# Row moments and the convolution's product set between B products on VectorE, and seven tanh set ahead of two copies on ScalarE

## The reference, cut to what matters

```
xn   = x * rsqrt(mean(x*x) + 1e-6) * norm_w
proj = xn @ W_in.T                       # x_branch (512), gate (512)
xc   = conv(x_branch, 4 taps) + conv_b
xc   = xc * sigmoid(xc)
dt   = soft_clamp(softplus(xc @ W_dt.T + b_dt), 0.001, 0.1, 0.5)
Bp, Cp = xc @ W_B.T, xc @ W_C.T          # 16 states each
dA   = exp(soft_clamp(dt * A, -8, 8, 0.5))
# over time t, for every (channel, state):
h    = h * dA[t] + dt[t] * Bp[t] * xc[t]
h    = h * min(20 / (norm(h) + 1e-8), 1) if t % 10 == 0
y[t] = sum over states(h * Cp[t]) + D_param * xc[t]
x    = layernorm(x + x + scale * ((y * gate * sigmoid(gate)) @ W_out.T))
```

## Time and profile before

| | us |
|---|---|
| three timed runs, median (lowest to highest) | 2796.52 (2795.47 to 2802.35) |
| the profiled execution | 2795.66 |
| its span, first to last instruction | 2793.6 |
| TensorE busy | 2601.1 (93%) |
| VectorE busy | 2397.1 (86%) |
| ScalarE busy | 2245.1 (80%) |
| GpSimd busy | 2132.6 (76%) |

### The profile page before, as it was taken

How to read it: one execution, slowest core, us unless ns; L and a number is a source line. 1 busy time by engine, 2 the same in 40 slices (tenths; PEclk the granted TensorE clock), 3 DMA queues, 4 the chain that set the end, 5 groups by cost and what they waited for, 6 DMA issues and landing times. The chain is left out here.

```text
span 2793.6 us, 50775 instructions
## 1 busy us (share of the span) xinstructions
PE 2601.1 (93%) x16812; PEld 2390.9 (86%) x16812; DVE 2397.1 (86%) x3391; ACT 2245.1 (80%) x5074; POOL 2132.6 (76%) x2237
## 2 busy tenths in 40 slices
PE   5899999999999999999999999999999976899992
PEld 4799999999999999999999999999999975677762
DVE  2899999999999999999999999999999997221224
ACT  5899999999999999999999999999999971111113
POOL 0788888888888888888888888888888883434314
PEclk9899999999999999999999999999999987999996
DMA  1222222222222222222222222222222222134226
GB/s 61 69 73 80 83 70 80 78 75 82 70 84 80 75 81 73 78 83 72 79 78 76 82 70 84 78 76 82 72 78 79 72 79 96 42 98 102 61 49 252
DMA packets 145746, 225.65 MB, mean 81 GB/s; under 512 B 37836, under 2 KB 84684, under 8 KB 144332
## 3 DMA queue, kind: packets, MB, share of 16 engines
q1 hardware_dynamic: 123044, 188.95, 22.1%
q0 software_dynamic: 9216, 12.59, 2.6%
q10 hardware_dynamic: 13224, 20.86, 2.2%
HBM read 189.27 MB, written 33.05 MB: 80 GB/s over the span
## 5 line engine op out<-in xcount | busy, mean ns | idle before, releaser
L792 POOL TENSOR_TENSOR H<-H,CB 128x640 f32<-128x640 f32 (+1 forms) x832 | 1216.8, 1477 | 199.9 <-DVE H L610 199.8
L610 DVE TENSOR_TENSOR_SCAN H<-DA,PM 128x704 f32<-128x704 f32 (+1 forms) x832 | 1309.9, 1595 | 0.0
L514 ACT ACTIVATE DA<-DT,SM 128x160 f32<-128x160 f32 (+1 forms) x3328 | 1107.0, 422 | 1.6 <-POOL DT L754 0.3
L815 PE MATMUL YB<-H,ID 128*128 128x160 f32 (+1 forms) x6656 | 1043.9, 309 | 0.0
L815 PEld LDWEIGHTS YB<-H,ID 128*128 128x128 f32 x6656 | 982.4, 191 | 16.0 <-issue 11.2
L579 DVE TENSOR_TENSOR PM<-PM,BB 128x640 f32<-128x640 f32 (+1 forms) x832 | 674.0, 810 | 0.0
L377 ACT ACTIVATE DA<-DA 128x2560 f32<-128x2560 f32 (+1 forms) x206 | 477.8, 2320 | 1.7
L821 PE MATMUL PAZ<-XN,RB 128*128 128x160 f32 x1664 | 254.9, 307 | 0.9 <-DVE VV L684 0.9
L831 PEld LDWEIGHTS PAZ<-XB,CD 128*128 128x128 f32 x1664 | 237.5, 188 | 16.8
L765 POOL TENSOR_TENSOR FC<-SN,HALF 128x4 f32<-128x4 f32 x206 | 232.9, 1130 | 21.3 <-DVE SN L617 7.1
L840 PE MATMUL PAZ<-XC,RB 128*128 128x160 f32 x1664 | 243.0, 299 | 3.9 <-DVE XC L645 3.9
(11 more groups left out here) (157 smaller groups left out, 2816.3 us busy)
## 6 DMA issues: line engine op xcount, KB each, us to landing
BB<-Bd SPq DMA_DIRECT2D x208, 320.0 KB, 3.4
CB<-Cd SPq DMA_DIRECT2D x208, 320.0 KB, 3.2
W<-in_w ACTq DMA_DIRECT2D x16, 1024.0 KB, 7.8
XT<-in_xT SPq DMA_DIRECT2D x52, 160.0 KB, 2.2
XR<-in_xp SPq DMA_DIRECT2D x208, 40.0 KB
X2d<-VV SPq DMA_DIRECT2D x208, 40.0 KB
YA<-VV SPq DMA_DIRECT2D x208, 40.0 KB
HI<-YA SPq DMA_DIRECT2D x6, 1024.0 KB, 9.9
```

The lines of the kernel that those rows point to most:

```text
L514: eng.activation(DA[:, c0 + k0:c0 + k1, :, a, m, 1:11].rearrange("p c b t -> p b c t"), DT[:, j % 2, a].rearrange("p b (c t) -> p b c t", ...
L610: eng.tensor_tensor_scan(H[:, q % 3, u, 0:n], decays(c, g)[:, u], DBX(u)[:, 0:n], 0.0, ALU.mult, ALU.add).then_inc(s_scan, 1)
L792: eng.tensor_tensor(h, h, cb, ALU.mult).then_inc(s_hc, 1)
L815: mm = eng.matmul(yv, ID[:], hv[:, :, :, n, 0:w], start=False, stop=n == 15)
```

## The change

Three edits, all in `ssm_phase`. The first changes ScalarE's table: step 0 deals seven tanh instead of three, and step 2 three instead of seven, so four tanh move ahead of the two copies of step 1. The second puts the first B product of a step in front of XC in step 6, where XC stood ahead of both. The third moves the row moments out of step 13: `bn_stats` stands in step 14 behind the first B product, and `bn_aggr` behind the second. GpSimd's, TensorE's and SyncE's programs stay as they are.

```diff
-            DUE = [0, 3, 3, 10, 12, 18, 19, 27, 35, 41, 43, 50, 56, 56, 58, 64, 64]
+            DUE = [0, 7, 7, 10, 12, 18, 19, 27, 35, 41, 43, 50, 56, 56, 58, 64, 64]
...
                     q = 4 * i + r
+                    if live and u % 2 == 0:
+                        mult(q, u)
                     if s == 6 and ok(i + 2):
                         j = i + 2
                         eng.wait_ge(s_th, j + 1)
...
+                    if s == 14 and ok(i - 1):
+                        j = i - 1
+                        eng.wait_ge(s_v, j + 1)
+                        for g in range(2):
+                            eng.bn_stats(BN[:, g], VV[:, g]).then_inc(s_bn, 1)
                     if live and u % 2 == 0:
-                        mult(q, u)
                         carry(q, u)
                         mult(q, u + 1)
+                    if s == 14 and ok(i - 1):
+                        eng.wait_ge(s_bn, 2 * i)
+                        if i > 1:
+                            eng.wait_ge(s_sd, i - 1)
+                        for g in range(2):
+                            eng.bn_aggr(MVR[:, g], BN[:, g]).then_inc(s_mv, 1)
                     if u == 2 and 1 <= q <= NQ - 2:
                         norm_sum(q - 1)
...
-                        eng.wait_ge(s_v, j + 1)
-                        for g in range(2):
-                            eng.bn_stats(BN[:, g], VV[:, g]).then_inc(s_bn, 1)
-                        eng.wait_ge(s_bn, 2 * (j + 1))
-                        if j > 0:
-                            eng.wait_ge(s_sd, j)
-                        for g in range(2):
-                            eng.bn_aggr(MVR[:, g], BN[:, g]).then_inc(s_mv, 1)
```

## The result

The changed kernel takes 2855.29 us (median, 2853.9 to 2857.11), the kernel before 2796.37 us in the same comparison: a ratio of 1.0206, with a 95% interval of 1.0189 to 1.0224. That is slower, as forecast, but by 59 us and not by 36; 2832 was too low and the range ended at 2848. The profiled execution took 2857.11 us, its span is 2855.0.

What follows compares the result with a forecast made beforehand. VectorE was taken to bound the kernel, with GpSimd's path from bn_aggr to CAR setting the time after the change: 2795.66 + 51.0 - 11.7 - 3.8 + 0.5 = 2831.7, or 2832 us; range 2822 to 2848.

Steps and rivals of the forecast that it cites:

- The bound: State-space pass of 43.25 us: VectorE, busy 43.18, has no room; ScalarE is level with it within 0.08 us.
- The stall at the copy of CAR: Step 0 of the next pass: VectorE waits 1.04 us for GpSimd's CAR, 49 times, 51.0 us.
- The gaps: VectorE's waits at bn_stats, bn_aggr and XC go: 0.31 us a pass saved, 15.5 us together.
- The rule of the Trainium skill that the prediction weighed: Rival at bn_stats and bn_aggr: waits cost nothing extra, so 11.7 us are not saved; 2844 us, chance 0.06.
- XC and the seven tanh: Step 6: XC no longer waits for ScalarE's tanh, covered by ScalarE's idle time; 0.08 us a pass, 3.8 us saved.
- GpSimd makes its 1.4 us up by step 4: GpSimd, 1.4 us later after the move, recovers from its 5.25 us of idle time; nothing is charged.
- The 0.5 us added for the end of the stage: Pass 51: short products put bn_aggr and the last two products of H some 0.5 us later; bounds 0 and 0.6.
- The upper bound of 2836: Top of the main forecast, 2829 to 2836 us by the bounds of hand-over and end, given chance 0.70.
- GpSimd's path to CAR: Rival: FC at step 14 meets the larger price, 0.2 us more in 49 passes; 2842 us, chance 0.10.
- TensorE waits 0.68 us a pass for XN: Projection starts some 0.6 us later, covered by 1.66 us of room; rival without cover: 2881 us, chance 0.04.
- The 0.69 us by which CAR came early: Before the change, VectorE reached the copy of CAR 6.32 us after bn_aggr, GpSimd's path took 5.63: 0.69 us to spare.

## Why the prediction was right and wrong

- **The bound.** VectorE's order sets the pass, before and after. Right: in every run the pass is VectorE's own work and what holds VectorE.
- **The stall at the copy of CAR.** Right in place, cause, size and number: VectorE idles 49.2 us in 50 passes, one of which is the wait of pass 51 that was there before (1.17 us; 1.16 now). That leaves 48.1 us in 49 passes, 0.98 each. With the 0.08 us by which the copy would start before the end of the product in front of it, it comes 1.06 us later, against 1.04. Earlier `bn_aggr` shortens it one for one.
- **The gaps.** 0.31 us a pass were expected, 0.36 are gone from VectorE's row starts (VV to the next row 0.69 to 0.58, the second `bn_stats` to the next 0.44 to 0.33, XC 0.08, the rest in the rows behind the moments). The rule of the Trainium skill that the prediction weighed (VectorE: DVE Perf Modes, "The DRAIN you can't avoid"), by which the waits cost nothing extra, doesn't hold in this case: the instruction behind VV starts 0.11 us sooner when it doesn't need VV. The same section also says that a next instruction that is not held starts earlier, and that agrees with the rows that start 0.08 to 0.09 us before an end.
- **XC and the seven tanh.** Right that ScalarE's idle time covers the tanh and that XC's wait goes. But the 0.08 us of a pass came back as a port wait in step 6 (0.50 to 0.57 us), and the 4 us that the two edits give lie mostly in passes 0 and 1, which I hadn't priced. The sum of 3.8 us was about right for another reason.
- **The step that failed** is "GpSimd makes its 1.4 us up by step 4 [...] I charge nothing for these". GpSimd was followed for who *waits* for it by semaphore: TensorE, ScalarE, the next CAR. All that held. It wasn't followed for whom it *gets in the way of*. Counted from VV, GpSimd is 1.4 us late at step 2 and VectorE only 0.8, which put GpSimd's product of H of step 1 on top of VectorE's product of DT and XC. Priced: 0.98 - 0.49 = 0.49 us in step 2 and 0.08 in step 6, 0.57 x 49 = 28 us. 2832 and 28 less the 3 us of the first passes make 2857, against 2855 measured. The 0.5 us added for the end of the stage don't show in the rows of VV: the last comes 49.9 us after the third last, 50.1 in the kernel before. The upper bound of 2836 doesn't follow from the bounds named for it, which reach to about 2832; that changes nothing here.
- **The other rivals.** GpSimd's path to CAR didn't get longer: FC takes 1.03 us at step 14 after the change as before. TensorE waits 0.68 us a pass for XN, as worked out (0.6), and has the room for it: in the middle of this stage nobody waits for TensorE in turn but ScalarE, which has idle time left.
- **The same rows were in hand.** The earlier trace rows show FC stretched from 1.03 to 1.21 us beside the product of DT and XC, and I used them for a rival in which GpSimd is slowed. The other direction, VectorE held by GpSimd, is the same conflict with the other one first, and the margin could be read there: the product started at 1206.46, GpSimd's product of H ended at 1206.52. The 0.69 us by which CAR came early had also kept these two apart. The change used that slack up, so both were lost at once. The conflict itself stood in the trace of the kernel before, once: in pass 50, where XC falls away and VectorE is early, the product took 1.30 us beside GpSimd's product of H and ended 0.35 us after it.

```profile
2254.37 1.49 POOL L792 TENSOR_TENSOR H<-H,CB 128x640 f32<-128x640 f32 x1
...
2254.91 1.30 DVE L566 TENSOR_TENSOR PM<-DT,XC 128x320 f32<-128x320 f32 x1
```

What makes the conflict is stated by the Trainium skill, SBUF — State Buffer, section "SBUF: two separate sides": VectorE and GpSimd share a pair of SBUF ports, and a VectorE instruction with two SBUF inputs and a GpSimd instruction that reads SBUF exclude each other for a whole instruction: the one that starts first keeps the ports, and the other waits. The traces agree: the product of DT and XC reads both inputs from SBUF and ends 0.36 us after GpSimd's instruction in the changed kernel and in the run with the early product; FC or the product of H is stretched when it comes second (1.21 and 1.58 us). The scans and B products, with one input in PSUM, run beside GpSimd's products of H without such a stretch (1.58 to 1.61 and 0.80 to 0.83 us in the changed kernel). That it is the port, and not another thing that excludes the same pairs, is the word of the Trainium skill; the runs show the exclusion.

## What to carry to other kernels

Before moving work behind a wait on a second engine, list what that engine has queued behind the wait, and who needs each of it. Then list a second time what that engine will be running while the first one comes to instructions that can't run beside it: a delay shifts both, by different amounts. An instruction that grows longer with no idle time in front of it, though nothing about it was changed, is the sign of it. And a saving of a few tenths of a microsecond is worth testing with the neighbours moved out of the way: here it turned from 59 us lost into 21 us won.

## What the runs showed of the hardware

- VectorE's product of two SBUF inputs (128x320) takes 0.47 to 0.50 us alone and, started while a GpSimd product of 1.5 us runs, ends 0.36 us after that one: 0.98, 1.32 and 1.44 us for starts 0.62, 0.96 and 1.08 us ahead of GpSimd's end. The profile counts it all as busy.
- In the other order GpSimd is held: FC takes 1.21 or 1.29 us instead of 1.03, the product of H 1.58 instead of 1.48. The end again follows that of the one that came first: FC ends 0.87 to 0.88 us after VectorE's product, the product of H 1.34.
- The hand-over from GpSimd to VectorE took 0.10 to 0.11 us (CAR done at 1230.01, copy at 1230.12), from ScalarE 0.03 to 0.04 us.
- A VectorE instruction that waits for the one in front of it starts 0.03 to 0.04 us after its end; one that doesn't starts 0.08 to 0.09 us before it.
